# A routed expert layer: token numbers written into the tile one-hots on VectorE, in place of a scaling of the lane one-hots on ScalarE

## The reference, cut to what matters

```
logits = h @ gate_weight.T; scores = sigmoid(logits)
... two best groups of four experts, then the four best experts of those; w = 2.5 * scores / sum
out    = sum over the 4 chosen experts e of  w_e * (silu(h @ g_e.T) * (h @ u_e.T)) @ d_e.T
shared = (silu(h @ sg.T) * (h @ su.T)) @ sd.T
return x + out + shared
```

## Time and profile before

| what | value |
|---|---|
| median of 3 runs | 828.82 us (828.13 to 833.23) |
| the profiled execution | 828.96 us |
| its span, first to last instruction | 827.2 us |
| mean granted TensorE clock | 0.999 |
| PE busy | 811.5 us, 98% of the span |
| ACT, DVE, POOL busy | 406.4, 481.9, 436.8 us |
| chain that ended last | PE 94%, ACT 2%, DVE 2%, DMA 1%, issue 1% |
| shared steps on PE | about 60 to 191 us |
| lane scaling on ACT | 104.5 to 149.7 us |

### The profile page before, as it was taken

One profiled execution on the slowest core, in us unless ns is written; L12 is line 12 of the kernel. 1 busy time (PEld: TensorE's weight loads), 2 busy tenths in 40 slices (PEclk: granted clock), 3 DMA queues, 4 the chain that ended last, 5 costly groups with the idle time before them and its releaser, 6 DMA issues.

```text
span 827.2 us, 19387 instructions
## 1 busy us (share of the span) xinstructions
PE 811.5 (98%) x4131; PEld 650.1 (79%) x4132; DVE 481.9 (58%) x1011; ACT 406.4 (49%) x814; POOL 436.8 (53%) x400
## 2 busy tenths in 40 slices
PE   9999999899999999999999999999999999999995
PEld 5577877787888888888888888888888888888874
DVE  5698887736544446744457446747557466464441
ACT  4864467535444335534356335536455355453441
POOL 5403111536467655566655656565465574775543
PEclk9999999999999999999999999999999999999999
DMA  8985967799999999799997999799998998997974
GB/s 290 391 330 179 244 162 196 168 257 262 226 266 234 183 192 191 185 264 240 203 197 182 270 229 206 197 270 189 234 269 161 279 253 193 252 213 157 188 112 66
DMA packets 145303, 181.50 MB, mean 219 GB/s; under 512 B 30570, under 2 KB 103922, under 8 KB 142834
## 3 DMA queue, kind: packets, MB, share of 16 engines
q0 software_dynamic: 37776, 89.08, 52.4%
q1 hardware_dynamic: 106528, 80.45, 37.7%
q10 hardware_dynamic: 834, 10.49, 3.4%
HBM read 82.52 MB, written 67.17 MB: 181 GB/s over the span
## 4 chain that ended last, share of the span: by engine, by line
PE 94%; ACT 2%; DVE 2%; DMA 1%; issue 1%; POOLq 0%; POOL 0%; ACTq 0%; SPq 0%; DVEq 0%
PE psGU L1119 47%; PE psY L1119 24%; PE psY L1177 4%; PE psH L996 4%; PE psGU L1160 3%; PE psGU L1162 3%; PE psGU L1161 3%; PE psT L996 1%; DMA raw_w<-ffn_w 1%; ACT x_ring L933 1%; PE psY L1045 1%; PE psGU L1045 1%; PE psH L1022 1%; PE psM L982 0%; PE psM L1147 0%
## 5 line engine op out<-in xcount | busy, mean ns | idle before, releaser
L1119 PE MATMUL psGU<-split_w,xT_pair 128*128 x1716 | 414.1, 390 | 1.6 <-issue 1.6
L1119 PEld LDWEIGHTS psGU<-split_w,xT_pair 128*128 128x128 f32 x1716 | 322.0, 188 | 70.2 <-issue 1.8
L696 POOL DMA_INDIRECT out<-y_ring,idx_all x143 | 227.8, 1593 | 202.0 <-SPq L582 180.7
L1751 DVE SCALAR_TENSOR_TENSOR aT<-aT,w_ring,psGU 128x256 f32<-128x256 f32 x143 | 68.7, 480 | 239.2 <-ACT aT L948 129.0
L691 POOL DMA_INDIRECT tok_ring<-h_rows,idx_all x143 | 154.4, 1080 | 69.9 <-issue 42.1
L1119 PE MATMUL psY<-split_w,hidT_hi 128*128 x564 | 187.4, 413 | 0.0
L948 ACT ACTIVATE aT<-psGU 128x256 f32<-128x256 f32 x143 | 55.0, 384 | 253.1 <-PE psGU L1119 197.6
L842 ACT ACTIVATE y_ring<-psY 128x512 f32<-128x512 f32 x173 | 103.1, 597 | 91.9 <-PE psY L1119 48.1
L1119 PE MATMUL psY<-split_w,hidT_lo 128*128 x282 | 111.1, 394 | 0.0
L1119 PEld LDWEIGHTS psY<-split_w,hidT_hi 128*128 128x128 f32 x564 | 95.4, 189 | 12.5 <-issue 0.2
L1736 DVE STREAM_TRANSPOSE psT<-x_ring 128x512 f32<-128x512 f32 x143 | 102.5, 717 | 0.9 <-DMA w_ring<-tok_ring 0.9
(11 more groups left out here) (261 smaller groups left out, 670.6 us busy)
## 6 DMA issues: line engine op xcount, KB each, us to landing
x_ring<-tok_ring SPq DMA_DIRECT2D x284, 128.0 KB
raw_w<-ffn_w SPq DMA_DIRECT2D x17, 1536.0 KB, 10.5
out<-y_ring POOLq DMA_DIRECT2D x32, 256.0 KB
x_ring<-x_pairs SPq DMA_DIRECT2D x12, 512.0 KB, 8.6
h_rows<-tok_ring SPq DMA_DIRECT2D x16, 256.0 KB, 9.6
h_rows<-y_ring SPq DMA_DIRECT2D x16, 256.0 KB, 9.5
tok_ring<-h_rows,idx_all POOLq DMA_INDIRECT x143
out<-y_ring,idx_all POOLq DMA_INDIRECT x143
```

Of the source, the lines that this page charges most:

```text
L696: pool.indirect_dma_start(out[:, :], bass.IndirectOffsetOnAxis(idx_all[:, r:r + 1], 0), y_ring[:, r % YRING, :], None, compute_op=ALU.add) ...
L1119: mm = pe.matmul(dst, a[:, slot, c], w(at + col + k * H), start=(k == 0 and a is high and at == 0), stop=(k == parts - 1 and a is low))
L1751: v.scalar_tensor_tensor(out=hid[:, half, :], in0=gate, scalar=w_ring[:, w_slot, bass.ds(expert, 1)], in1=up, op0=ALU.mult, op1=ALU.mult). ...
```

## The change

The token's number moves from the lane one-hots to the tile one-hots, where DVE had a multiplication already. `scale_lanes`, its steps and its semaphore go; PE now waits for DVE's multiplication alone (`entry_ready`, one for each g). `slot_scale` becomes `slot_value`: 1 for an even tile, 2^-12 for an odd one, multiplied once, at n = 11, by the token's number, which now runs from -2048 to 2047 and may be zero. In `make_entries` the compare for `lane1h` is now counted by `put`, so `settle()` waits for it too before the multiplication. Since zero is a token now, pads are found in another way: an expert's slots end at `start * 128 + count`, its limit. DVE copies the counts (n = 7), makes the limit as a thirteenth row of the expert table (n = 9), spreads it on 16 partitions (`limits`, n = 14), PE multiplies it with `running` at n = 16 into `psT[1]` (a limit for each tile on all partitions), and a new piece "pads" at n = 19 makes the pad rows from it in four instructions. `fill_idx` is rewritten: five instructions where there were seven.

```diff
-ODD = 6144.0
+ODD = 2.0 ** -12
...
-               16: ("read_words",), 23: ("fill_idx",), 24: ("read_sp_words",)}
+               16: ("read_words",), 19: ("pads",), 23: ("fill_idx",), 24: ("read_sp_words",)}
...
-SCALE_STEPS = {13: (0,), 14: (1,), 15: (2, 3), 16: (4, 5), 17: (6, 7), 18: (8, 9), 19: (10, 11), 20: (12, 13),
-               21: (14, 15)}
...
-        ROWS = 12
+        ROWS = 13
...
-                    iota(token_no[:, 0:mid], [[P, mid]], -N // 2, 1)
-                    iota(token_no[:, mid:NT], [[P, mid]], 1, 1)
+                    iota(token_no[:], [[P, NT]], -N // 2, 1)
...
-                for e in SCALE_STEPS.get(n, ()):
-                    scale_lanes(e)
...
-            def scale_lanes(g):
-
-                act.wait_ge(places_ready, 2 * (g + 1))
-                s = g % ENTRY_RING
-                half = PAIRS // DUO // ENTRIES
-                for k in range(ENTRIES):
-                    lanes = lane1h[:, s, k * half:(k + 1) * half, :, :].rearrange("p d l q -> p (d l q)")
-                    act.activation(lanes, lanes, ACT.Copy, scale=token_no[:, g * ENTRIES + k:g * ENTRIES + k + 1]
-                                   ).then_inc(entry_ready, 1)
...
+            def spread_limits():
+
+                pe.wait_ge(limits_ready, 1)
+                pe.matmul(psT[1][:, NRP:2 * NRP - 1], limits[:], running[:], start=True, stop=True
+                          ).then_inc(limits_spread, 1)
...
-                pe.wait_ge(entry_ready, ENTRIES * (g + 1))
+                pe.wait_ge(entry_ready, g + 1)
...
                     sp_table()
+                    spread_limits()
...
+                put(v.tensor_copy(count_e[:], total))
...
+                stt(limit, start, float(P), count_e[:], ALU.mult, ALU.add)
...
+                v.tensor_scalar(limits[:], ones[0:E, :], col(LIMIT), None, ALU.mult).then_inc(limits_ready, 1)
...
-                put(v.tensor_copy(slot_scale[:], part_i[:, 2, :]))
-                settle()
-                ts(slot_scale[:], slot_scale[:], (ODD - 1.0) / P, 1.0, ALU.mult, ALU.add)
+                put(v.tensor_copy(slot_value[:], part_i[:, 2, :]))
+                settle()
+                ts(slot_value[:], slot_value[:], (ODD - 1.0) / P, 1.0, ALU.mult, ALU.add)
+                settle()
+                values = slot_value[:].rearrange("p (c k) -> p c k", k=TOPK)
+                tt(values, values, spread(token_no[:], TOPK), ALU.mult)
                 settle()
...
-                v.tensor_tensor(lane1h[:, s], every(lane_q[:]), duos(slot_lane[:, pairs], P), ALU.is_equal
-                                ).then_inc(places_ready, 1)
-                settle()
-                v.tensor_tensor(entry[:, s], entry[:, s], duos(slot_scale[:, pairs], NRD), ALU.mult
-                                ).then_inc(places_ready, 1)
+                put(v.tensor_tensor(lane1h[:, s], every(lane_q[:]), duos(slot_lane[:, pairs], P), ALU.is_equal))
+                settle()
+                v.tensor_tensor(entry[:, s], entry[:, s], duos(slot_value[:, pairs], NRD), ALU.mult
+                                ).then_inc(entry_ready, 1)
+
+            def pad_places():
+
+                v.wait_ge(limits_spread, 1)
+                pads = table_pad[:].rearrange("p n q -> p (n q)")[:, 0:NR]
+                ts(pads, psT[1][:, NRP:2 * NRP - 1], part_no[:, 0:1], 1.0 / P, ALU.subtract, ALU.mult)
+                settle()
+                tt(pads, pads, iota_tile[:, 0:NR], ALU.is_le)
+                settle()
+                tt(pads, pads, pad_rows[:, 0:NR], ALU.mult)
+                settle()
+                ts(pads, pads, float(N // 2), None, ALU.add)
+                settle()
...
-                ts(odd, psM[:, 0:NRD], 1.0 / ODD, ROUND, ALU.mult, ALU.add)
...
+                both = psM[:, 0:NRD]
+                ts(evens[:], both, ODD / 2, ROUND, ALU.add, ALU.add)
+                settle()
+                ts(evens[:], evens[:], -ROUND, None, ALU.add)
+                settle()
+                tt(odds[:], both, evens[:], ALU.subtract)
+                settle()
+                stt(idx_two[:, 0:NR // 2, 1], odds[:, 0:NR // 2], 1.0 / ODD, table_pad[:, 0:NR // 2, 1], ALU.mult, ALU.add)
+                v.tensor_tensor(idx_two[:, :, 0], evens[:], table_pad[:, :, 0], ALU.add).then_inc(slots_ready, 1)
```

More of the change, by code:

```diff
@@ L273, in build @@
         n_used = sb("n_used", [P, 1])
-        ROWS = 12
+        ROWS = 13
+        count_e = sb("count_e", [P, E])
         e_rows = sb("e_rows", [P, ROWS, E])
@@ L278, in build @@
         (USED, NOT_LAST, START, END, TURN, PREP, PREP_END,
-         ACT_K, DVE_K, PE_K, ACT_MORE, DVE_MORE) = range(ROWS)
+         ACT_K, DVE_K, PE_K, ACT_MORE, DVE_MORE, LIMIT) = range(ROWS)
         sp_raw = sb("sp_raw", [P, E])
@@ L290, in build @@
         prep_ends = in_x([E, NRP])
+        limits = in_x([E, P])
         takes = sb("takes", [E, E + SPLITS + 2])
@@ L303, in build @@
         slot_lane = sb("slot_lane", [P, NT * TOPK], F16)
-        slot_scale = sb("slot_scale", [P, NT * TOPK], F16)
+        slot_value = sb("slot_value", [P, NT * TOPK], F16)
         with nc.sbuf_tensor("entry_high", [P, ENTRY_RING * PAIRS * NRP // 2], F32R) as entry_high:
@@ L310, in build @@
         in_cw_late = home(cw_ring[:].rearrange("p s c -> p (s c)"), RING * P)
[L311 to L315, removed]
+        evens = in_cw_late([P, NRD])
+        odds = in_cw_late([P, NRD])
+        table_pad = in_cw_late([P, NRD, 2])
+        idx_all = sb("idx_all", [P, NRP], U32)
+        idx_two = idx_all[:].rearrange("p (n q) -> p n q", q=2)
         psT = [ps(f"psT{i}") for i in range(2)]
@@ L366, in build @@
         sp_words_ready = sem("sp_words_ready")
-        places_ready = sem("places_ready")
+        limits_ready = sem("limits_ready")
+        limits_spread = sem("limits_spread")
         entry_ready = sem("entry_ready")
@@ L626, in _ @@
             pool.sem_inc(consts, 1)
-            mid = NT // 2
             def late_const(m):
@@ L1449, in _ @@
             used, not_last, start, end, turn, prep, prep_end = [e_rows[:, k, :] for k in range(7)]
-            act_k, dve_k, pe_k, act_more, dve_more = [e_rows[:, k, :] for k in range(7, ROWS)]
+            act_k, dve_k, pe_k, act_more, dve_more, limit = [e_rows[:, k, :] for k in range(7, ROWS)]
             (rank, used2, big, e0, span, tmp, third, turn2, before_start, key, base, level, is_last
@@ L1651, in fill_idx @@
             def fill_idx():
                 v.wait_ge(table_done, N_GROUPS)
-                even, odd = table_both[:, :, 0], table_both[:, :, 1]
-                ts(odd, psM[:, 0:NRD], 1.0 / ODD, ROUND, ALU.mult, ALU.add)
+                both = psM[:, 0:NRD]
+                ts(evens[:], both, ODD / 2, ROUND, ALU.add, ALU.add)
                 settle()
-                ts(odd, odd, -ROUND, None, ALU.add)
+                ts(evens[:], evens[:], -ROUND, None, ALU.add)
                 settle()
-                stt(even, odd, -ODD, psM[:, 0:NRD], ALU.mult, ALU.add)
+                tt(odds[:], both, evens[:], ALU.subtract)
@@ L1660, in fill_idx @@
                 settle()
-                stt(table_up[:], table[:], 0.0, table[:], ALU.is_gt, ALU.subtract)
-                stt(table_pad[:], table[:], 0.0, pad_rows[:, 0:NR], ALU.is_equal, ALU.mult)
-                settle()
-                ts(table_up[:], table_up[:], -1.0, float(N // 2), ALU.mult, ALU.add)
-                settle()
-                v.tensor_tensor(idx_all[:], table_up[:], table_pad[:], ALU.add).then_inc(slots_ready, 1)
+                stt(idx_two[:, 0:NR // 2, 1], odds[:, 0:NR // 2], 1.0 / ODD, table_pad[:, 0:NR // 2, 1], ALU.mult, ALU.add)
@@ L1817, in route_part @@
                         read_sp_words()
+                    elif part == "pads":
+                        pad_places()
                     elif part == "fill_idx":
```

## The result

The changed kernel takes 825.32 us (median of 13 runs, 823.78 to 826.86) against 828.71 us for the kernel before on the same chip (13 runs, one of which took 4639.82 us; the median doesn't feel it). The ratio is **0.9956 [0.9944, 0.9969]**: 0.44% faster, which is less than the 1% that one measurement tells from no change, but its interval lies clear of 1. The change was timed twice more among the experiments: 0.9975 [0.996, 0.999] and 0.997 [0.9951, 0.9989]. The forecast was 824.7 in 822.7 to 828.5, and within 1%, so both were right. The profiled execution has a span of 823.5 us at clock 0.998.

What follows compares the result with a forecast made beforehand. PE bounds the kernel, busy 98% of the span, so only its stops can pay. From 828.96, less 4.55, plus 0.3 and 0.05, gives 824.76; with the median 0.14 lower, about 824.7 us, range 822.7 to 828.5.

Steps and rivals of the forecast that it cites:

- Four stops: PE's stops at 105, 128, 145 and 149 us in the shared steps; all vanish, gaining 4.55 us.
- spread_limits: New two-pass float32 matmul on PE, 143 columns: charged 0.3 us, bounds 0.24 and 0.6.
- The 22.8 us: ACT's lane scaling, 32 instructions of 712 ns, counted as 22.8 us of ACT work taken out.
- The margin at n = 12: DVE's low part ends 0.45 us before PE's down product; new DVE work charged 0.05, bounds 0 and 0.3.
- The wait in each pass: DVE's multiplication now waits for the lane compare's end: 0.13 us a pass, 2.1 in all over 16.
- Groups 12 and 13: One-hots for PE's table fill, at the third stop: ready near 141.5, PE asks at 142.5, so the stop goes.
- The pads: Four chained DVE operations of 143 elements at n = 19: 1.2 us.
- Rival A: Part of the stops stays, or a new one opens at n = 12 or 20: 826.9 us; chance 0.14.
- C: Rival: DVE becomes the bound through the added wait in `make_entries`, about 0.5 more a pass: 829.6 us; chance 0.04.
- The first routed gate product: Start of PE's routed tiles: comes near 187.1 us instead of 191.26.
- Rival B: The start of the routed tiles doesn't move, held by gathers: 825.6 us if only 0.9 is lost; chance 0.07.
- the routed stage repeats at PE's own pace and carries the gain to the end: Routed tiles after the shared steps: same pace for each tile, gain kept to a span of about 823 us.

Runs made afterwards that it cites:

- e9: e6's kernel repeated unchanged: the changed kernel with ACT only waiting for DVE's one-hots at the old steps, no scaling; 830.52 us, ratio 0.9999.
- e11: The changed kernel a third time, no edit, as the mark for its set; 826.8 us, ratio 0.997 to the kernel before.
- e3: The changed kernel plus 32 idle ACT copies with the old waits at the old scaling steps; 832.74 us, ratio 1.0035 to the kernel before.
- e1: The changed kernel again, no edit; 826.85 us, ratio 0.9975 to the kernel before.
- e7: The changed kernel with DVE's multiplication no longer waiting for the lane compare, which counts for PE instead; 828.39 us, ratio 0.9966 to the kernel before.
- e2: The changed kernel with the head of DVE's loop placed elsewhere, DVE_HEAD 93 for 77; 824.83 us, ratio 0.9949 to the kernel before.
- e5: The kernel before with ten tiny DVE memsets at the start, moving DVE's later code; 830.28 us, ratio 1.0008 to the kernel before.
- e8: The changed kernel with the edits of e2 and e7 together; 827.37 us, ratio 0.9965 to the kernel before.
- e4: The changed kernel with e3's idle ACT work at other steps, no down copy queued right behind; 826.07 us, ratio 0.9964 to the kernel before.
- e6: The changed kernel with ACT only waiting for DVE's one-hots at the old steps, no scaling; 830.14 us, ratio 0.9999 to the kernel before.
- e12: The kernel before with one more small matmul and its wait ahead of PE's routed-tile loop; 829.2 us, ratio 0.9991 to the kernel before.
- e10: The changed kernel with e6's bare ACT waits moved to e4's steps; 826.34 us, ratio 0.9962 to the kernel before.

## Why the prediction was right, and where it was lucky

- **Four stops go, 4.55 us.** Right: no stop is left. With the new costs on PE, 0.35 as charged, the forecast for the shared steps was 4.2; 4.19 came. That it came so close is luck in part, as two misses of about 0.2 cancel (see `spread_limits` below).
- **What they were made of.** The prediction put the down copies' lateness on the scalings ahead of them. That is only part of it: e9 has the waits, with the transfer's issue behind them, but no scalings, and takes 3.0 us more between the marks than e11; e3, with waits and copies, takes 5.7 more than e1. How the 4.2 us of the kernel before divide isn't measured, since DVE's entries come earlier there. The 22.8 us are also the sum of records that overlap: ACT's busy time fell by 17.3. The chain of work on ACT was read rightly, but ACT's idle time ahead of it (a scaling that waits for DVE's entries) was not costed. Here it made no difference, since the change removes both.
- **`spread_limits`, 0.3.** Measured 118.70 - 118.27 = 0.43, within its bounds. **The margin at n = 12, 0.05:** measured about 0.10; PE's first pair of down matmuls at 100.85 takes 0.56 instead of 0.46. Together 0.18 too little was charged, so the stops held about 0.2 more than the 4.55 counted.
- **The wait in each pass, 0.13.** 0.12 measured, and e7 takes it back. The Trainium skill ("VectorE: DVE Perf Modes", The DRAIN you can't avoid) says that a semaphore between DVE instructions costs nothing extra; the trace does not agree for this pair. The same page's section Two Vector instructions with no wait between them says that an instruction that it calls held starts only when every earlier one has finished. e7's multiplication starts at 103.90, 0.09 before the compare's end, so it is not held, and the wait alone makes the 0.12.
- **Groups 12 and 13, the tightest place.** Forecast 141.5 against 142.5. DVE's multiplication of group 13 ends at 141.46 and PE fills at 142.56. The pads took 130.18 to 131.53, 1.35 for a forecast of 1.2. Rival A had no place here, and C needed four times the 0.12.
- **The first routed gate product, 187.1.** It came at 186.76 on the chain (191.26 before), of which 0.31, by the first mark, is an earlier first stage and not shown to be the change's. Rival B falls: the gathers had their numbers at about 149 instead of 154.4, and PE had no wait there.
- **Failed: "the routed stage repeats at PE's own pace and carries the gain to the end".** It gave back 0.8 net in the profile. The largest part is the 1.36 of DVE's stand at its loop's entry (shown by e2, e5 and e8), which is a cost of the change that no list of its operations contains: some seven more instructions in DVE's code. That the span came out as forecast (823) is luck: it rests on the earlier first stage (0.31) and on the 0.93 of PE's loop exit, which varies from execution to execution and was no term of the forecast. The three ratios of the changed kernel, 0.9956, 0.9970 and 0.9975, mean gains of 2.1 to 3.6 us, less than the 4.1 forecast, as that loss would have it; the medians alone don't show that it is the cause.

## What to carry to other kernels

A copy that frees a bank for PE should have nothing in front of it in its engine's queue, neither work nor a wait for a slower engine; what must be there is better moved to a step where no such copy is due; here 32 instructions of ACT cost nothing there. Read an engine's idle time ahead of late work as well as the work, and don't trust the releaser's name where the named engine was done before. And when a change adds instructions ahead of a loop, look at the first turns of that loop in the new trace: where the code lies is a term of the sum.

## What the runs showed of the hardware that was not expected

- DVE stood 4.9 to 6.0 us, against 2.3 in the middle of all tiles, where it enters its loop, in all ten profiles in which its code had been moved (with the head still at 77), and in none of the four others. Stands of 4.1 to 6.4 us came at tile 130 too, in e2, e4, e6, e8 and e12, so the other place of the head doesn't rid DVE of all of them. The Trainium skill ("Runtime: NRT & Kernel Launch", Instruction fetch mechanics) says that a jump to code that isn't in the engine's buffer waits until it is loaded; the place of the stand agrees. The trace's DMA view goes with it: in all ten profiles a packet of the instruction queue q14 moved 2.3 to 4.5 us before the product that ends the stand, and in the four others none in that stretch. Whose code such a packet carries the view doesn't say, and at tile 130 there are such packets with and without a stand, so that the loading makes the stand is likely and not shown.
- PE stood 0.69 to 2.21 us at its loop's exit. The changed kernel gave 0.69 to 0.72 in its three profiles, but e6's kernel, with the same code on PE, gave 0.74 and, as e9, 1.24, and e10's 2.21. What sets it stays open.
- The granted clock fell to the level of 1.2 GHz for about 3.7 us within the shared steps in one profile (e6), and not in the repeat of the same kernel (e9); with the code the same in both, this is scatter, and e6 takes 1.64 us more between the marks than e9.
- The same program's stage of routed tiles took 638.4 us in one profile (e9) and 641.7 in another (e6), and its tiles took 4.337 and 4.353 us. Times between two marks on PE told differences of 0.1 us, where the medians of whole runs told 1 to 2.
